# Attention of an audio tower on one core: fp32 operands on row halves of the array, instead of split operands on the whole of it

## The reference

```python
h = tok(x, ...)                       # 8 recurrent steps over shifted tokens, width 64
# attention: layernorm twice (the second with ln_scale), 8 heads of width 64
Q, K, V = xn @ W_q[h], xn @ W_k[h], xn @ W_v[h]
sqdist  = maximum(q2 + k2 - 2.0 * Q @ K.T, 0.0)      # q2, k2: row sums of squares
scores  = exp(-gamma[h] * sqdist)                     # no normalization
h = h + concat_heads(scores @ V) @ W_o.T
h = h + ffn(layernorm(h), ...)        # 16 experts, top 2, F = 128, then layernorm
```

## Time and profile before

| | |
|---|---|
| median of the runs | 867.75 us (866.63 to 869.34, 3 runs) |
| the profiled execution | 868.95 us |
| its span, first to last instruction | 866.5 us |
| mean granted TensorE clock | 0.981 of full speed |
| busy: PE, DVE, ACT, POOL | 89%, 81%, 62%, 53% of the span |

### The profile page before, as it was taken

One profiled execution on the slowest core, in us unless ns is written; L12 is line 12 of the kernel. 1 busy time (PEld: TensorE's weight loads), 2 busy tenths in 40 slices (PEclk: granted clock), 3 DMA queues, 4 the chain that ended last, 5 costly groups with the idle time before them and its releaser, 6 DMA issues.

```text
span 866.5 us, 17080 instructions
## 1 busy us (share of the span) xinstructions
PE 767.8 (89%) x5712; PEld 451.4 (52%) x5712; DVE 703.0 (81%) x1809; ACT 534.5 (62%) x1042; POOL 461.9 (53%) x628
## 2 busy tenths in 40 slices
PE   2999889999999999999999989988888888888893
PEld 1444456666666666666666655344444444444441
DVE  3676679999999999999999977877777777777762
ACT  1565678888778878787887775444444444544342
POOL 8642254454444453544534421566667667676666
PEclk9999989999999999999999998999999999999997
DMA  6300022211112211122111220000000000000000
GB/s 161 103 2 2 1 49 50 50 39 36 35 41 50 50 26 37 38 50 50 38 37 30 46 50 1 3 1 7 7 8 7 10 11 8 7 8 7 8 7 18
DMA packets 22861, 25.71 MB, mean 30 GB/s; under 512 B 12888, under 2 KB 21720, under 8 KB 22648
## 3 DMA queue, kind: packets, MB, share of 16 engines
q1 hardware_dynamic: 21608, 23.57, 11.7%
q10 hardware_dynamic: 1168, 1.07, 0.5%
HBM read 5.30 MB, written 2.43 MB: 9 GB/s over the span
## 4 chain that ended last, share of the span: by engine, by line
PE 52%; DVE 35%; issue 6%; ACT 3%; POOL 2%; ACTq 1%; DMA 1%; DVEq 0%; POOLq 0%
DVE prob L783 15%; PE bank L1183 9%; PE bank L1204 9%; DVE m L799 9%; PE bank L1068 6%; PE bank L996 6%; PE bank L1116 6%; PE bank L1092 3%; PE bank L1094 2%; DVE qk L793 2%; DVE top L896 2%; PE bank L1195 2%; PE bank L1237 2%; PE bank L986 1%; DVE wtok L907 1%
## 5 line engine op out<-in xcount | busy, mean ns | idle before, releaser
L783 DVE TENSOR_SCALAR prob<-prob,cap_hi,cap_lo 125x250 f32<-125x250 f32 x512 | 234.3, 505 | 22.9 <-ACT prob L539 20.1
L405 POOL TENSOR_TENSOR sq<-sq 125x256 f32<-125x256 f32 x128 | 96.1, 756 | 171.7 <-ACT sq L553 126.3
L442 POOL TENSOR_TENSOR gated<-relu,wb 128x500 f32<-128x500 f32 x96 | 123.8, 1294 | 96.8 <-ACT relu L629 96.7
L539 ACT ACTIVATE prob<-bank 125x500 f32<-125x500 f32 x256 | 148.8, 592 | 38.6 <-PE bank L1094 35.5
L914 DVE SCALAR_TENSOR_TENSOR gated<-bank,nb,wb 128x500 f32<-128x500 f32 x160 | 116.9, 733 | 67.9 <-PE bank L1183 67.8
L1204 PE MATMUL bank<-gated,w_sb 64*64 64x500 f32 x1024 | 167.2, 589 | 0.0
L1183 PE MATMUL bank<-cs,w_sb 64*64 64x500 f32 x1024 | 164.1, 581 | 0.7 <-DVE gated L914 0.5
L629 ACT ACTIVATE relu<-bank,b_sb 128x500 f32<-128x500 f32 x96 | 64.7, 674 | 124.2 <-PE bank L1183 123.2
L1068 PE MATMUL bank<-prob,u 125*64 125x250 f32 x1024 | 127.1, 385 | 1.3
L1092 PE MATMUL bank<-m,s 128*125 128x500 f32 x256 | 111.2, 434 | 6.3 <-issue 6.3
L1094 PE MATMUL bank<-m,s 112*125 112x500 f32 x256 | 101.6, 397 | 0.0
(11 more groups left out here) (169 smaller groups left out, 1346.2 us busy)
## 6 DMA issues: line engine op xcount, KB each, us to landing
m<-m SPq DMA_DIRECT2D x128, 125.0 KB, 2.3
out<-res SPq DMA_DIRECT2D x16, 125.0 KB
xa<-xparts SPq DMA_DIRECT2D x4, 281.2 KB
w_sb<-in_w SPq DMA_DIRECT2D x1, 1024.0 KB
xw<-xparts SPq DMA_DIRECT2D x4, 140.6 KB
w_sb<-in_w SPq DMA_DIRECT2D x1, 512.0 KB
m<-s SPq DMA_DIRECT2D x32, 15.6 KB
xparts<-x_part SPq DMA_DIRECT2D x1, 375.0 KB, 5.0
```

Source lines behind the costliest of these rows:

```text
L442: gp.tensor_tensor(gated[g % 8][:, :], relu_sb[n % 3][:, :], wb[q % 2][:, :], ALU.mult).then_inc(c_gatep, 1)
L539: act.activation(prob[n % PROBS][:, :, :], bank[5 + n % 3][0:T, 0:C].rearrange("p (h l) -> p h l", h=2), ACT.Exp).then_inc(b_exp, 1)
L783: last = dve.tensor_scalar(part, part, cap_hi[0:T, h:h + 1], cap_lo[0:T, h:h + 1], ALU.min, ALU.max)
```

## The change

Stage B is written anew; A and C stay, but for one residual instruction that is now one instead of two.

- Operands are unsplit fp32. `xT` holds the transposed tokens on both row halves. Eight matmuls (four chunks, two column halves) replace the four transposes, and one ACT copy follows instead of two ACT roundings and a DVE instruction.
- A unit is two matmuls over 64 rows, on row half LO into bank 2 and on HI into bank 3: q beside k, head beside head, chunk beside chunk. There are eight units per pair, one in each slot. Banks 2 and 3 are the only ones, so unit k waits until unit k-1 is evacuated. ACT squares both banks for q and k; for G and `u` ACT copies bank 2 and DVE bank 3. DVE reduces the squares at their full width; POOL's fold is gone, as are `m2`'s rest and the eight DMAs of `duplicate`.
- Scores of a slot are four fp32 matmuls and four bf16 matmuls over 64 rows, two heads in two banks (4 + 2(v%2) + a), both key chunks in each. A bank has one head, so DVE caps with one instruction of 125 x 500. The rank terms are three bf16 parts, made on POOL by six instructions (`row_parts`), moved by eight bf16 matmuls, one DVE copy into `s2` and six DMAs of one destination row each.
- Projections begin two slots earlier than before (`unit_at`: units 0 and 1 of pair p+1 in slots 6 and 7 of step p).
- The orders are new. PE: `fold_b` first in slot 2, `rows_b` first in slot 5, then scores, unit, products, and `tokens_b(p+1)` last in slot 3, which waits for `b_res` of pair p-2. ACT: exponentials, unit, `evac_y` last in slots 1 and 5. DVE: caps with the squares between them, unit, `residual` last in slot 3.

```diff
+        xT = [sb(f"xT{j}", [128, C]) for j in range(3)]
+        m2 = [sb(f"m2_{j}", [128, H, C], BF16) for j in range(2)]
+        s2 = [sb(f"s2_{j}", [128, C], BF16) for j in range(2)]
...
+        def slots(slot):
+            for p, v in [(-1, 6), (-1, 7)] + [(p, v) for p in range(PAIRS + 1) for v in range(8)] + [(PAIRS + 1, 0), (PAIRS + 1, 1)]:
+                slot(p, v)
+        def unit_at(p, v):
+            n = 8 * p + v + 2
+            return divmod(n, 8) if 0 <= n < 8 * PAIRS else (0, None)
+        def ev_until(n):
+            p, k = divmod(n, 8)
+            return 12 * p + (2 * k if k < 4 else k + 4), 4 * p + max(0, k - 4)
+        def score_bank(v, a):
+            return bank[4 + 2 * (v % 2) + a][0:T, 0:C].rearrange("p (c l) -> p c l", c=2)
...  SP
-            steps(step_b)
+            for p in range(PAIRS):
+                sp.wait_ge(b_s2, p + 1)
+                wait(sp, b_sc, 16 * (p - 1))
+                for half in (0, HALF):
+                    for r in range(PARTS):
+                        sp.dma_start(m2[p % 2][half + r:half + r + 1, :, :],
+                                     s2[p % 2][half + Q_ROW + r * H:half + Q_ROW + (r + 1) * H, :]).then_inc(b_row, 16)
...  POOL: row_parts(p) is six instructions on 125 x 64 values, each waiting for the one before
+            b_scales(0)
+            for p in range(PAIRS):
+                if valid(p + 1):
+                    b_scales(p + 1)
+                row_parts(p)
...  ACT
+            def unit(p, k):
+                act.wait_ge(b_pj, 8 * p + k + 1)
+                if k < 4:
+                    for a in range(2):
+                        n = 2 * k + a
+                        wait(act, b_red, 8 * p + n - 3)
+                        act.activation(sq[n % 4][:, :, :], bank[2 + a][0:T, :].rearrange("p (h d) -> p h d", h=H), ACT.Square)\
                             .then_inc(b_ev, 1)
+                elif k < 6:
+                    wait(act, b_sc, 16 * (p - 1))
+                    act.activation(m1[p % 2][:, 2 * (k - 4), :], bank[2][:, 0:C], ACT.Copy).then_inc(b_ev, 1)
...
+            def slot_b(p, v):
+                if valid(p - 1):
+                    exps(p - 1, v)
+                if v == 4 and valid(p + 1):
+                    tokens_b(p + 1)
+                q, k = unit_at(p, v)
+                if k is not None:
+                    unit(q, k)
+                if v == 1 and valid(p - 2):
+                    evac_y(p - 2, 1)
+                if v == 5 and valid(p - 1):
+                    evac_y(p - 1, 0)
...  DVE
+            def slot_b(p, v):
+                q, k = unit_at(p, v - 1)
+                for a in range(2):
+                    if valid(p - 1):
+                        cap(p - 1, v, a)
+                    if k is not None and k < 4:
+                        squares(q, 2 * k + a)
+                q, k = unit_at(p, v)
+                if k is not None and k >= 4:
+                    unit(q, k)
+                if v == 3 and valid(p - 2):
+                    residual(p - 2)
+                if v == 5 and valid(p):
+                    rows_b(p)
+                if v == 4 and valid(p + 2):
+                    norm_stats(p + 2, b_ln)
...  PE
+            def fold_b(p):        # four fp32 matmuls of 64 columns, after b_y, b_s2 and b_res
+            def scores(p, v):
+                b, hp = v // 4, v % 4
+                wait(pe, b_exp, 16 * p + 2 * v - 2)
+                if v == 0:
...
+                    pe.wait_ge(b_row, 96 * (p + 1))
...
+                for c in range(2):
+                    for a, rows in ((0, LO), (1, HI)):
+                        pe.matmul(score_bank(v, a)[:, c, :], xT[p % 3][rows, keys[c]], m1[p % 2][rows, hp, queries],
+                                  start=True, stop=False)
+                    for a, rows in ((0, LO), (1, HI)):
+                        last = pe.matmul(score_bank(v, a)[:, c, :], s2[p % 2][rows, keys[c]],
+                                         m2[p % 2][rows, 2 * hp + a, queries], start=False, stop=True)
...
+            def unit(p, k):
...
+                evs, evd = ev_until(8 * p + k)
+                wait(pe, b_ev, evs)
+                wait(pe, b_evd, evd)
+                for a, rows in ((0, LO), (1, HI)):
+                    if k < 4:
+                        last = pe.matmul(bank[2 + a][0:T, :], x[rows, k * T:(k + 1) * T], wqk_sb[rows, :],
+                                         start=True, stop=True)
...
+            def slot_b(p, v):
+                if v == 2 and valid(p - 2):
+                    fold_b(p - 2)
+                if v == 5 and valid(p):
+                    rows_b(p)
+                if valid(p - 1):
+                    scores(p - 1, v)
+                q, k = unit_at(p, v)
+                if k is not None:
+                    unit(q, k)
+                if v == 0 and valid(p - 2):
+                    products(p - 2, 6)
+                    products(p - 2, 7)
+                if v in (2, 4, 6) and valid(p - 1):
+                    products(p - 1, v - 2)
+                    products(p - 1, v - 1)
+                if v == 3 and valid(p + 1) and p >= 0:
+                    tokens_b(p + 1)
```

More of the change, by code:

```diff
@@ L322, in _ @@
             assert count[0] == PREP_GA
-            for j in range(2):
-                done(gp.memset(f32(m2[j][64:96, :, :]), 0.0))
             done(gp.memset(qkw[:, :, :], 0.0))
@@ L525, in _, with tokens_b @@
                 body_a(i)
-            round_b(0, 0)
+            def tokens_b(p):
+                act.wait_ge(b_xt, p + 1)
+                wait(act, b_sc, 16 * (p - 2))
+                act.activation(xT[p % 3][:, :], bank[0][:, 0:C], ACT.Copy).then_inc(b_x, 1)
             def evac_y(p, b):
@@ L581, in start_c @@
+            tokens_b(0)
             def start_c(v):
@@ new lines, in _, with residual, cap @@
+            norm(1, b_ln)
+            def residual(p):
+                rows = h_all[:, p * CH:(p + 1) * CH, :]
+                dve.wait_ge(b_f, p + 1)
+                dve.tensor_tensor(rows, bank[0][0:T, 0:CH * D].rearrange("p (c d) -> p c d", c=CH), rows, ALU.add)\
+                    .then_inc(b_res, 1)
+            def cap(p, v, a):
+                n = 2 * v + a
+                h = n % H
+                dve.wait_ge(b_exp, 16 * p + n + 1)
+                part = prob[n % PROBS][:, :, :]
+                dve.tensor_scalar(part, part, cap_hi[0:T, h:h + 1], cap_lo[0:T, h:h + 1], ALU.min, ALU.max)\
+                    .then_inc(b_cap, 1)
@@ new lines, in rows_b @@
+            def rows_b(p):
+                dve.wait_ge(b_qt, p + 1)
+                wait(dve, b_sc, 16 * (p - 1))
+                dve.tensor_copy(s2[p % 2][:, :], bank[0][:, 0:C]).then_inc(b_s2, 1)
+            def slot_b(p, v):
+                q, k = unit_at(p, v - 1)
+                for a in range(2):
+                    if valid(p - 1):
[11 more added lines that the diff above has]
+                    norm_stats(p + 2, b_ln)
+                if v == 6 and valid(p + 2) and p >= 0:
+                    norm_aggr(p + 2, b_ln)
+                if p == PAIRS - 1 and v == 0:
@@ L956, in group_c @@
                     result(p - 2)
-            steps(step_b_tail)
+            slots(slot_b)
             for g in range(12, 16):
@@ L1046, in tokens_b @@
                 pe.wait_ge(b_xn, p + 1)
[L1047 removed]
+                wait(pe, b_res, p - 2)
+                wait(pe, b_s2, p - 1)
                 for c in range(CH):
[L1049 to L1050 removed]
+                    for rows in (LO, HI):
+                        last = pe.matmul(bank[0][rows, c * T:(c + 1) * T], xn[:, c, :], ident[0:T, 0:T],
+                                         start=True, stop=True)
                 last.then_inc(b_xt, 1)
@@ new lines, in unit @@
+            def unit(p, k):
+                x = xT[p % 3]
+                if k == 0:
+                    pe.wait_ge(b_x, p + 1)
+                if p == 0 and k == 0:
+                    pe.wait_ge(ld_b, 16 * len(B_LOADS))
+                    for n in range(LANES):
+                        pe.wait_ge(a_h[n], ROUNDS)
+                evs, evd = ev_until(8 * p + k)
[4 more added lines that the diff above has]
+                        last = pe.matmul(bank[2 + a][0:T, :], x[rows, k * T:(k + 1) * T], wqk_sb[rows, :],
+                                         start=True, stop=True)
+                    elif k < 6:
+                        h = 2 * (k - 4) + a
+                        last = pe.matmul(bank[2 + a][:, 0:C], wg_sb[rows, h * 128:(h + 1) * 128], x[rows, :],
+                                         start=True, stop=True)
+                    else:
+                        c = 2 * (k - 6) + a
+                        last = pe.matmul(bank[2 + a][0:T, :], x[rows, c * T:(c + 1) * T], wu_sb[rows, :],
+                                         start=True, stop=True)
+                last.then_inc(b_pj, 1)
@@ new lines, in rows_b @@
+            def rows_b(p):
+                pe.wait_ge(b_qw, 6 * p + 6)
```

(11 more changed lines are left out.)

434 lines of the change are left out of this document (107 added, 327 removed).

## The result

The changed kernel takes 966.72 us (median of 4 runs, 963.58 to 970.45) against 868.3 for the kernel before (4 runs, 866.63 to 869.34): 1.1137 times as long, 95% interval 1.1087 to 1.1188. Forecast were 966.1, with a range of 898 to 1005. The profiled execution took 963.58 us, its span is 961.8, its mean granted clock 0.962.

What follows compares the result with a forecast made beforehand. PE was taken to bound the kernel: 26.8 us of stream plus 5.8 of waits per step. Prologue 29.3, steps 479.1, last step 26.4, C 326.5, start 95.0 and clock 8.5 gave span 964.8, time 966.1 us, range 898 to 1005.

Steps and rivals of the forecast that it cites:

- prologue: Start of stage B: units unable to overlap their evacuation, row DMAs and 2 us for the clock, 29.3 us.
- the clock's term: Fifteen steps of stage B: five stretches of PE at half clock in all, 8.5 us.
- last step: End of stage B: left at 26.4 us, since it sits on the experts' first chain.
- the waits: PE in each step: four waits of 1.7, 2.2, 0.8 and 1.1 us from written orders, 5.8 us together.
- PE's stream: PE's own work per step: units 6.9, scores 8.8, products 8.2, the rest 2.9, sum 26.8 us.
- The change of shape and back: PE, switching to another array shape and back: costs 0.29 us; row half to column half costs the same.
- The three short visits: PE's tokens, fold and rows per step: 1.2, 1.15 and 0.55 us, each including 0.29 for the shape change.
- The rival in which they take turns: PE's row halves do not overlap: units 1.72, scores 2.2, 15.7 us more per step, 1200 us; chance 0.04.
- Half of the waits: Rival for the steps: evacuations run earlier, small DMAs land early, 43 us less, 923 us (895 to 935); chance 0.15.
- faster, by packing: Rival for the steps: waits vanish, PE streams at column count, 25.1 us a step, 855 us; chance 0.09.
- 2.5 come back as wait for the rank rows: Fifteenth step: 6.0 us shorter without tokens and new units, of which 2.5 return as waiting for rank rows.
- Edits at nothing: DVE, ACT and POOL work and the dropped duplicate DMAs: no gain, covered by PE, unless PE were shorter.

Runs made afterwards that it cites:

- e5: Changed kernel with evac_y first in slot 1, residual first in slot 3, copies of rank rows and unit 7 first in slot 5: 872.72 us.
- e9: e8 with the token matmuls behind slot 0's products, as in e6, and DVE's copy of unit 5 first in slot 3: 858.69 us.
- e3: Changed kernel with the fold's matmuls on PE behind the products of slot 2 instead of first in it: 934.13 us.
- e7: Changed kernel without the fp32 score matmuls on row half HI, the bf16 part kept: 994.76 us.
- e1: Changed kernel with DVE's residual ahead of the caps in slot 3: 937.52 us.
- e2: Changed kernel with ACT's evac_y ahead of the exponentials in slot 1: 930.71 us.
- e4: Changed kernel with DVE's copy of the rank rows into s2 ahead of the caps in slot 5: 963.21 us median, 949.6 to 974.31.
- e8: e5 with the first pair's units in the prologue alternating between banks 2, 3 and banks 4, 5: 864.41 us.
- e6: e5 with the token matmuls moved behind the products of slot 0 and ACT's token copy to slot 1: 879.75 us.

## Why the prediction was right

The time came within 1 us of the forecast, which is partly luck: its terms are off by up to 6 us in both directions, and within the steps two errors of 16 and 10 us largely cancel. Against the forecast span of 964.8 us the measured 961.8 is made up so:

| | forecast | measured |
|---|---|---|
| prologue | 29.3 | 32.5 |
| fifteen steps and the clock's term | 479.1 + 8.5 | 481.8 |
| last step | 26.4 | 27.7 |
| C | 326.5 | 324.8 |

In the second row the waits and PE's stream were too large and the clock's term too small: without up to 18.7 us for eleven stretches at half clock, 463.1 are left for the 479.1. A full step at full clock is 31.46 us, forecast 32.5.

Around the span lie 1.8 us (2.45 taken), and the profiled execution is 3.1 us below the median (1.2 above was taken), which closes the rest of the gap.

**What bounds.** The forecast costed PE first and found that it alone needs a whole step of before: right. PE's stream is 26.46 us by e5, forecast 26.8, and a step of before 26.5. By part: scores 1.06 us a slot (1.10), a unit 0.86 (0.86), products 1.84 until the next group starts. The change of shape and back came out at its 0.29: 1.84 - 1.75 = 0.09 in the products' own row, 0.09 ahead of them (a unit takes 0.95 before products and 0.86 before scores), 0.10 in the scores behind (1.16 against 1.06), and e9 finds 0.27 for one that falls away. The three short visits were given a full 0.29 each; only the rows' was too dear (0.32 us instead of 0.55), since they follow the products, which are on column halves as they are. That row halves to column halves is no cheaper than from the full array was open in the forecast; the measured steps bear it out, and e3 adds that column halves to full columns is no cheaper either. The rule of the Trainium skill that was weighed there ("TensorEngine Tiling (Array Packing)", Key Properties: a change of tiling mode drains the engine, a change of tile alone does not) agrees with these rows, and with the products' 1.74 us where other work on column halves follows, against 1.84.

**Overlap of row halves.** Full, as rows 5 and 6 had it; e7 shows that the second half of the scores costs nothing. The rival in which they take turns is out.

**The waits.** All four are there, in their places and at nearly their sizes:

| wait | forecast | measured | shown by |
|---|---|---|---|
| tokens on the residual | 2.2 | 1.84 | e1 |
| fold on `evac_y` | 1.7 | 1.54 | e2, e3 |
| scores of slot 0 on the row DMAs | 1.1 | 0.80 | e4 |
| unit 0 on the copy of unit 7 | 0.8 | 0.49 | e5 |

The sum is 4.67 instead of 5.8, and the term that was mis-sized is the same in three of them: the chain on DVE. I took 0.60 us from one DVE instruction of 500 columns to the next, from a line that reads PSUM; caps read SBUF, and two of them take 1.02 us together at 333.42, of which each is 0.54 long, so they start some 0.48 apart. The residual starts 2.34 us after the scores' end (332.60 to 334.94), forecast 2.65. The chain on ACT, taken from rows 9, was exact: `evac_y` starts at 357.48, 2.10 us after the scores' end at 355.38, forecast 2.12. The rank rows' chain too was right as a whole (8.5 us from the scores' end at 341.80 to 350.26, forecast 8.75), the DMAs taking 5.41 us from the first issue at 344.85, where 5.4 was taken between bounds of 5.0 and 5.8. "Half of the waits" and "faster, by packing" fall by this table.

**The clock** is the step that failed most, though inside its range: eleven stretches at half clock between the copies, not five, up to 18.7 us instead of 8.5. It hid the too large waits. The Trainium skill's rule that the prediction weighed ("TensorE: Matmul & The Clock Gate", Part 1: idle gaps between bursts, longer than any here, bring the half clock) would have given none. The trace disagrees with it as a full account: no wait in the full steps is over 1.9 us, and the clock fell in them. The prediction left out that the same Part has a second case, in which short idles between groups of matmuls, if they come often, make the clock go down and up; with that the trace agrees. This is one of the places (it answers rows 12):

```profile
353.00:356.40 3.40, 3.40 (x30) 1.00 0.00 0
356.40:359.80 3.40, 1.86 (x17) 1.00 0.00 0
359.80:363.20 3.40, 3.40 (x16) 0.53 0.00 0
363.20:366.60 3.40, 3.40 (x28) 0.97 0.00 0
```

A stretch with 1.86 of 3.4 us of work, the wait before the fold among it, then half clock for 3.4 us. It shows where the clock fell and is no rule: from 332.7 to 336.1 us, over the wait for the residual, PE was busy 1.55 of 3.4 us, and the clock stayed at full behind it.

**The prologue** was 3.2 us longer than forecast. The form of the sum was right (a unit, then 1.18 to 1.2 us of wait for its single pair of banks; forecast 0.2 + 0.48 + 0.6 + 0.1 = 1.38), but 2 us for the clock were far too few: it is 0.69 over the prologue, and the units of 101 to 115 us run at half of it (the first four units and their waits take 12.1 us, 98.81 to 110.89, forecast 9.0). e8 confirms the mechanism from the other side.

**The last step** was left at 26.4 us and took 27.7. The wait that the forecast named for the fifteenth step ("2.5 come back as wait for the rank rows") is there, at its end, with 3.12 us:

```profile
609.32 1.20 PE L1030 MATMUL bank<-m,xT 64*125 64x250 f32 x4 [3.12 <-DMA m<-s]
```

Without new units to do, PE reaches the scores of slot 0 before the rank rows have landed. In e9, where their copy goes first, the stretch from the last copy into `s2` to the first matmul of C is 30.8 us (501.6 to 532.35) against 33.8 (603.2 to 637.0).

**Edits at nothing** cost nothing while PE waited. In e5, with PE full, they still don't: DVE is busy 66% of its steps. The statement "if PE were shorter, these would show again" is borne out by e6: with the tokens' 1.0 us gone from between units 5 and 6, a wait of 0.52 on DVE came out.

## What to carry to other kernels

Before costing a change of operands, write out PE's stream in order with what each entry waits for: here the new arithmetic by itself was worth nothing per full step (26.46 us of stream against steps of 26.5), and four instructions that stood late in their slots on other engines were worth 94 us in all. An evacuation, a copy or a residual on which an in-order PE waits belongs ahead of the bulk work of its slot, and single banks leave no room for it to be late. A wait on PE can cost more than itself, since a stretch at half clock behind it costs up to 1.7 us more: in e2 taking away 22 us of waits gave 34. It need not: in e1 24 us gave 27. And compare steps at full clock with each other before crediting an edit with what the clock did.

## What the runs showed of the hardware

- The granted clock fell to half in steps whose longest wait is 1.9 us (after 3.4 us of which PE was busy 1.86, above), nine times in the full steps of the changed kernel, and not once between the copies in e5, where the longest wait of a full step is 0.2 us and PE is busy 98% of the time.
- Leaving one row half idle during the scores lowered the mean clock from 0.96 to 0.91 at the same busy share (e7). Whether the rows in use or the number of instructions matter, these runs don't tell.
- Going to another shape of the array and back cost 0.27 us where e9 saved it. Column halves to the full array costs as much as to row halves (1.84 us for the products either way, e3); between two uses of column halves with other operands it is 0.1 less (products to rows 1.74).
- DMAs of 7.8 KB into one destination row cost SyncE 0.63 us each to issue, about as much as those of 15.6 KB (0.70, rows 10) and of 125 KB (0.59, L275) in the kernel before:

```profile
L276 SPq DMA_DIRECT2D m<-s x96: 625/629/1589, 122.1 to 607.3; - x96
```
